# Experts' results written in quarters, the second attention's preparation moved forward, and the normed tokens stored chunk first

## The reference

```python
x = x + tanh(g_xattn[0]) * attention0(layernorm(x), ctx, ctx)
x = x + tanh(g_ffn[0])   * experts(layernorm(x))
x = x + tanh(g_xattn[1]) * attention1(layernorm(x), ctx, ctx, mask)
x = x + tanh(g_ffn[1])   * squared_relu_mix(layernorm(x))
```

```python
grouped  = x.reshape(b, s // 32, 32, d)            # 128 groups of 32 tokens in all, 16 a batch
logits   = einsum('bntd,des->bntes', grouped, Wc) + bc + tie
perm     = (logits == max over the group's tokens) # each of 128 experts picks a token of each group
permuted = einsum('bntd,bntes->bnesd', grouped, perm)
inner    = relu(einsum('bnesd,esdf->bnesf', permuted, W1) + b1)   # f = 32
result   = einsum('bnesf,esdf->bnesd', inner, W2) + b2
out      = einsum('bnesd,bntes->bntd', result, perm)
```

## Time and profile before

| | before |
|---|---|
| median of 3 runs | 1328.79 us |
| profiled execution, own time | 1330.8 us |
| its span, first to last instruction | 1329.0 us |
| PE / DVE / ACT / POOL busy | 95% / 67% / 43% / 42% |
| mean granted clock of TensorE | 0.983 of full speed |
| HBM read / written | 129.92 / 82.62 MB |

### The profile page before, as it was taken

The page is one execution under the profiler, slowest core; times in us unless marked ns, Lnnn a source line. Parts: engine busy times, 40 slices in busy tenths (PEclk is TensorE's granted clock), DMA queues, the critical chain, the costliest instruction groups (busy, mean ns, idle before and its releaser), DMA issues.

```text
span 1329.0 us, 28238 instructions
## 1 busy us (share of the span) xinstructions
PE 1258.5 (95%) x10607; PEld 905.9 (68%) x10607; DVE 887.9 (67%) x1570; ACT 571.1 (43%) x1039; POOL 553.9 (42%) x456
## 2 busy tenths in 40 slices
PE   9999999999999978887999999999997999999998
PEld 7777776777677657621446666766775778888887
DVE  6985786777666555564546766766675977777762
ACT  4255345534552554453562443344246433333331
POOL 3313642454251100000339666865834644544540
PEclk9999999999999998998899999999998999999999
DMA  9875455324421678899983653563414111111101
GB/s 350 219 184 191 154 154 174 109 80 149 141 76 33 207 207 273 287 399 362 401 340 117 221 171 94 175 220 120 131 53 159 64 63 63 63 40 54 63 27 37
DMA packets 126502, 213.59 MB, mean 161 GB/s; under 512 B 27609, under 2 KB 49369, under 8 KB 122331
## 3 DMA queue, kind: packets, MB, share of 16 engines
q1 hardware_dynamic: 126427, 212.57, 48.1%
HBM read 129.92 MB, written 82.62 MB: 160 GB/s over the span
## 4 chain that ended last, share of the span: by engine, by line
PE 76%; DVE 9%; DMA 5%; ACT 4%; issue 3%; SPq 2%; POOL 1%; ACTq 0%; DVEq 0%; POOLq 0%
PE b L157 12%; PE b L158 11%; PE b L159 11%; PE b L1585 5%; PE b L1783 5%; PE b L1784 4%; PE b L1785 4%; PE b L1557 4%; PE b L1690 3%; PE b L2113 3%; PE b L2079 3%; PE b L1698 2%; ACT a_pr L1149 2%; PE b L2097 2%; PE b L1605 2%
## 5 line engine op out<-in xcount | busy, mean ns | idle before, releaser
L1149 ACT ACTIVATE a_pr<-b 120x512 f32<-120x512 f32 x252 | 130.1, 604 | 95.3 <-PE b L1585 95.3
L1338 DVE TENSOR_REDUCE a_mx<-b 128x4 f32<-128x480 f32 x256 | 152.0, 652 | 10.3 <-PE b L1557 10.2
L1031 POOL TENSOR_TENSOR a_rp<-a_rp,a_b2s 128x512 f32<-128x512 f32 x96 | 120.4, 1290 | 24.8 <-DMA a_rp<-s_rp 24.8
L1070 POOL TENSOR_TENSOR a_atl<-a_pvs,a_ath 128x512 fp32r<-128x512 f32 x64 | 81.1, 1301 | 81.8 <-ACT a_ath L1193 81.8
L1783 PE MATMUL b<-a_woh,a_ath 128*128 128x512 f32 x256 | 105.2, 411 | 3.1 <-POOL a_atl L1070 3.1
L157 PE MATMUL b<-a_xth,a_wqh 128*128 128x512 f32 x256 | 103.7, 405 | 0.8 <-DVE a_wql L825 0.5
L1784 PE MATMUL b<-a_wol,a_ath 128*128 128x512 f32 x256 | 102.3, 400 | 0.0
L1785 PE MATMUL b<-a_woh,a_atl 128*128 128x512 f32 x256 | 102.2, 399 | 0.0
L159 PE MATMUL b<-a_xth,a_wql 128*128 128x512 f32 x256 | 101.2, 395 | 0.0
L158 PE MATMUL b<-a_xtl,a_wqh 128*128 128x512 f32 x256 | 101.1, 395 | 0.0
L1483 DVE SCALAR_TENSOR_TENSOR a_x<-b,a_gate,a_x 128x512 f32<-128x512 f32 (+1 forms) x64 | 47.8, 747 | 72.2 <-PE b L1785 72.2
(11 more groups left out here) (245 smaller groups left out, 3142.7 us busy)
## 6 DMA issues: line engine op xcount, KB each, us to landing
a_rp<-s_rp SPq DMA_DIRECT2D x128, 256.0 KB, 4.6
s_x<-a_x SPq DMA_DIRECT2D x16, 1024.0 KB, 4.3
s_rp<-e_chosen SPq DMA_DIRECT2D x16, 1024.0 KB, 7.1
s_rp<-e_xc SPq DMA_DIRECT2D x16, 1024.0 KB, 7.5
e_w<-in_w SPq DMA_DIRECT2D x56, 256.0 KB, 5.1
a_xr<-in_x_t SPq DMA_DIRECT2D x8, 1024.0 KB, 6.6
a_x<-in_x SPq DMA_DIRECT2D x8, 1024.0 KB, 10.5
s_xn<-a_xn SPq DMA_DIRECT2D x8, 1024.0 KB, 4.7
```

Of the source, the lines that this page charges most:

```text
L1031: pool.tensor_tensor(rp[:, t, a], rp[:, t, a], b2s[:, :], ALU.add).then_inc(rp_biased, 1)
L1149: act.activation(pr[:, h % RING, :], bank[k][0:S2, :], ACT.Exp, scale=SCALE)\
L1338: dve.tensor_reduce(mx[:, t, :, r], bank[k][:, 0:HJ * S2].rearrange("p (a s) -> p a s", a=HJ), AX.X, ALU.max).then_inc(free[k], 1)
```

## The change

Four things change together.

1. `s_xn` is laid out [chunk, partition, tile, 128], and the first attention's `xn` [128, chunk, tile, 128]; a quarter of a chunk is then read in pieces of 4 KB. DVE writes with strides, and the transposes and the gather's last lhs read accordingly. Chunk 2's tokens are loaded at c = 1, s = 0 to 3, after the step's block of W1, no longer at c = 0.
2. A result step takes a quarter of the groups (32, two batches): eight products with 32 rows and 32 columns, four for each of two banks. The first 8 stores are batches 0 and 1 of all experts, the other 24 the remaining three quarters by 16 experts at a time. The experts keep their natural order.
3. `load_behind`: perm of batch 0, b2 and gates at u = 5, batch 0's reads at u = 9 after the first 8 stores have landed (`front_written`), keys and `bo` at u = 11, batch 1's perm and reads at u = 31. The steps move: merge 27, weights 29, norm 32, queries 34, 36, 38, 40, maxima 36 to 43, rows 46.
4. In turn 0 of the second attention the merges of batch 1 on PE stand later: 0 and 1 after scores 2, 2 and 3 after values 1.

```diff
-MERGE_AT, WEIGHT_AT, NORM_AT, QUERIES_AT, ROWS_AT = 41, 43, 45, (47, 49, 51, 53), 58
-MAXIMA_AT = {49 + n: (n // 2, (0, 1) if n % 2 == 0 else (2, 3)) for n in range(8)}
+MERGE_AT, WEIGHT_AT, NORM_AT, QUERIES_AT, ROWS_AT = 27, 29, 32, (34, 36, 38, 40), 46
+MAXIMA_AT = {36 + n: (n // 2, (0, 1) if n % 2 == 0 else (2, 3)) for n in range(8)}
...
-        of = 0 if isinstance(j, int) and j < HALF else 1
-        src = io["rp"][of].rearrange("u (c j a t) s d -> (u c) s j t a d", c=2, a=GT, t=NT)
+        src = io["rp"].rearrange("u c j (a t) s d -> (u c) s j t a d", a=GT)
         for a in range(GT):
-            sp.dma_start(rp[:, t, a:a + 1], src[:, :, bass.ds(j - HALF * of, 1), t, a]).then_inc(rp_in[t], 16)
+            sp.dma_start(rp[:, t, a:a + 1], src[:, :, bass.ds(j, 1), t, a]).then_inc(rp_in[t], 16)
...
-        if u == 7:
+        if u == 5:
             load_perm(sp, 0)
             sp.dma_start(b2[:, :], io["b2"]).then_inc(w_in[2], 16)
             load_gates(sp)
             sp.dma_start(bq[:, :], io["bq"]).then_inc(c_in, 16)
-        if u == HALF_U:
-            front.half_written(sp)
+        if u == FRONT_U:
+            front.front_written(sp)
             for t in range(NT):
                 load_experts(sp, 0, t)
             load_query_weight(sp)
-        if u == HALF_U + 2:
+        if u == FRONT_U + 2:
             sp.wait_ge(const, 2)
             load_keys(sp, 0)
             sp.dma_start(bo[:, :], io["bo"].partition_broadcast(P)).then_inc(bo_in, 16)
-        if u == 22:
+        if u == EK - 1:
             for k, uses in TW:
                 sp.wait_ge(full[k], uses.n(None, "merge", 1) + 1)
             load_perm(sp, 1)
@@ -890,7 +888,7 @@
         if u == 28:
             load_v(sp, 0)
 
-    HALF_U = EK // 2
+    FRONT_U = EK // 4 + 1
 
     def sync(sp):
         if route:
@@ -904,7 +902,8 @@
             sp.dma_start(b2s[:, :], io["b2"]).then_inc(b2_in, 16)
...
-            sp.dma_start(tokens(io["xn_out"][i - 1]), xn[:, :, :]).then_inc(xn_st, 16)
+            sp.dma_start(io["xn_out"][:, :, bass.ds((i - 1) * NT, NT), :].rearrange("c p t d -> p c t d"),
+                         xn[:, :, :, :]).then_inc(xn_st, 16)
...
+            late = merging and first_turn(i)
+            if merging and not late:
                 merge_tile(i, i + 1, 0)
                 merge_tile(i, i + 1, 1)
             scores(i, i, 1)
-            if merging:
+            if merging and not late:
                 merge_tile(i, i + 1, 2)
             values(0)
-            if merging:
+            if merging and not late:
                 merge_tile(i, i + 1, 3)
             if merge and last_:
                 pe.wait_ge(free["t"], TB.n(B - 2, "mt", 0) + 1)
                 pe.wait_ge(free["w"], W.n(B - 2, "o", 1) + 1)
                 after[0].transposes(pe, None, (0, 1))
             scores(i, i, 2)
+            if late:
+                merge_tile(i, i + 1, 0)
+                merge_tile(i, i + 1, 1)
             values(1)
             if merge and last_:
                 after[0].transposes(pe, None, (2, 3))
+            if late:
+                merge_tile(i, i + 1, 2)
+                merge_tile(i, i + 1, 3)
...
-    def expert(k, a):
-
-        q, c = divmod(a, 2)
-        return 8 * (k // 2) + 4 * c + 2 * (k % 2) + q
+    def round_of(u):
+
+        if u < EK // 4:
+            return 0, u
+        return 1 + (u - EK // 4) % 3, (u - EK // 4) // 3
 
     def result_on_act(p, q):
 
-        return q == 0 or (p >= EK and (p % 2 == 1 or MERGE_AT < p <= NORM_AT))
+        return q == 0 or (p >= MERGE_AT and (p % 2 == 1 or MERGE_AT < p <= NORM_AT))
...
-        sp.dma_start(xc[c % 2][:, q * XQ:(q + 1) * XQ], io["xn"][q * XQ:(q + 1) * XQ].rearrange(
-            "n p d -> p n d")[:, :, c * P:(c + 1) * P]).then_inc(x_in[c % 2][q], 16)
+        tiles = slice(q * XQ, (q + 1) * XQ)
+        sp.dma_start(xc[c % 2][:, tiles], io["xn"][c, :, tiles]).then_inc(x_in[c % 2][q], 16)
...
-                if s % 2 and c + 2 < C:
-                    load_tokens(sp, c + 2, s // 2)
                 if c:
                     sp.wait_ge(h_full[s % 2], (SETS * (c - 1) + s) // 2 + 1)
                     load_w1(sp, WG * (c - 1) + s + RW)
+                if c == 1 and s < 4:
+                    load_tokens(sp, 2, s)
+                if c == 1 and s % 2:
+                    load_tokens(sp, 3, s // 2)
...
-            sp.dma_start(io["rp"][2 * u // EK][u % (EK // 2)], slot(u)).then_inc(out_st[u % RO], 16)
+            h, n = round_of(u)
+            sp.dma_start(io["rp"][n, :, 2 * h:2 * h + 2].rearrange("c j g e d -> c (j g) e d"), slot(u))\
+              .then_inc(out_st[u % RO], 16)
-    def half_written(sp):
+    def front_written(sp):
         for q in range(RO):
-            sp.wait_ge(out_st[q], 16 * (EK // 2 // RO))
+            sp.wait_ge(out_st[q], 16 * (EK // 4 // RO))
...
-            k, h = p % EK, p // EK
-            if k % 4 == 0:
-                pe.wait_ge(relued, k // 4 + 1)
-            if k % KS == 0:
-                pe.wait_ge(w2_in[k // KS], 16 * KS)
+            h, n = round_of(p // 2)
+            if h == 0 and p % 2 == 0:
+                pe.wait_ge(relued, n + 1)
+                if n % 2 == 0:
+                    pe.wait_ge(w2_in[n // 2], 16 * KS)
             for q in range(2):
-                b, n = result_bank(p, q)
-                pe.wait_ge(g_free[b], n)
-            for a in range(EJ):
-                rows, (q, c) = slice(a * EF, (a + 1) * EF), divmod(a, 2)
-                b, _ = result_bank(p, q)
-                ins = pe.matmul(gbank[b][c * NH:(c + 1) * NH, :], inner[rows, k, h * NH:(h + 1) * NH],
-                                w2[k // KS][rows, k % KS, :], start=True, stop=True, skip_group_check=True)
-                if c:
-                    ins.then_inc(g_full[b], 1)
+                b, use_of = result_bank(p, q)
+                pe.wait_ge(g_free[b], use_of)
+            for c in range(4):
+                for q in range(2):
+                    a, k = 2 * (p % 2) + q, 4 * n + c
+                    rows, (b, _) = slice(a * EF, (a + 1) * EF), result_bank(p, q)
+                    ins = pe.matmul(gbank[b][c * NQ:(c + 1) * NQ, :], inner[rows, k, h * NQ:(h + 1) * NQ],
+                                    w2[k // KS][rows, k % KS, :], start=True, stop=True, skip_group_check=True)
+                    if c == 3:
+                        ins.then_inc(g_full[b], 1)
...
-        b, n = result_bank(EK + number * KS - 1, 1)
+        last = max(u for u in range(EK) if round_of(u)[1] < 2 * number)
+        b, n = result_bank(2 * last + 1, 1)
...
-    rp_d = [dram(f"s_rp{i}", (EK // 2, P, EJ, D)) for i in range(2)]
+    rp_d = dram("s_rp", (EK // 4, 4, B, GB, EJ, D))
```

More of the change, by code:

```diff
@@ L74 @@
              ("a1_pvs", (0, 4 * KB), "f_tmp"), ("e_b1", (0, 400), "f_mu f_gate f_stats f_mv f_mark f_ve f_rstd")]
-HALF = B // 2
 Engines = namedtuple("Engines", "sync gpsimd scalar vector tensor")
@@ L593, in attention @@
         atl=([P, C, T], F32R), pvs=([P, C, T], F32), mt=([P, T], F32R), rs=([P, TQ], F32), rx=([P, TQ], F32R),
-        xn=([P, NT, D], F32), x=([P, XS, NT, D] if route else [P, XS, X_SPAN // 4], F32), xr=([P, C, T], F32), mr=([P, 2 * T], F32), wch=([P, C, ES], F32R),
+        xn=([P, C, NT, P] if route else [P, NT, D], F32), x=([P, XS, NT, D] if route else [P, XS, X_SPAN // 4], F32), xr=([P, C, T], F32), mr=([P, 2 * T], F32), wch=([P, C, ES], F32R),
         wcl=([P, C, ES], F32R), bcol=([P, 1], F32), tie=([P, G], F32), lg=([P, T], F32), gmax=([P, GB], F32),
@@ L1293, in apply @@
             for t in range(NT):
-                dve.tensor_scalar(to[:, t, :], x[:, t, :], mv[:, t, 0:1], rstd[:, t:t + 1],
+                if route:
+                    out, of = to[:, :, t, :], x[:, t, :].rearrange("p (c d) -> p c d", c=C)
+                else:
+                    out, of = to[:, t, :], x[:, t, :]
+                dve.tensor_scalar(out, of, mv[:, t, 0:1], rstd[:, t:t + 1],
                                   ALU.subtract, ALU.mult).then_inc(normed, 1)
@@ L1524, in second_norm @@
                 for t in range(NT):
-                    last = pe.transpose(bank[k][:, t * P:(t + 1) * P], xn[:, t, c * P:(c + 1) * P],
-                                        ident[:, :])
+                    last = pe.transpose(bank[k][:, t * P:(t + 1) * P], xn[:, c, t, :], ident[:, :])
                 last.then_inc(full[k], 1)
@@ L1843, in experts @@
     RB, RO, KS, RW = 6, 4, 8, 4
-    NH = NG // 2
+    NQ = NG // 4
     EARLY = 2
@@ L1933, in load_ahead @@
             tiles = slice(NTILE - 2 * NT, NTILE - NT)
-            sp.dma_start(xc[0][:, tiles], io["xn"][tiles].rearrange("n p d -> p n d")[:, :, 0:P]).then_inc(x_in[0][3], 16)
+            sp.dma_start(xc[0][:, tiles], io["xn"][0, :, tiles]).then_inc(x_in[0][3], 16)
         else:
@@ L2077, in gather @@
                 b, _ = use(SETS * c + s, a)
-                lhs = xc[c % 2][rows, TS * s + t, :] if tokens is None else tokens[rows, t, 0:P]
```

(10 more changed lines are left out.)

5 lines of the change are left out of this document (2 added, 3 removed).

## The result

The changed kernel takes 1561.51 us (median of 4 runs, 1557.83 to 1563.18), the kernel before 1329.54 beside it: a ratio of 1.1729, 95% interval 1.1702 to 1.1757. That is 232 us slower. The forecast, its range (1320 to 1341) and all four rivals missed it.

A forecast was written before the change was run, and what follows sets the result against it. PE bound the gather, the DMA queue the results stage; 560.3 - 5.9 + 28.6 + 34.2 + 28.3 + 31.5 + 13.6 + 2.1 = 692.7 for batch 1's merges, +2.5 at turn's end: median 1331.3, range 1320 to 1341 with rivals 1 to 3.

The forecast's parts named there:

- stores run at 417 GB/s, 2.51 us per MiB: Results stage: store price read from the profile before, used for the changed kernel's stores too.
- rival 3: Reads of results slow down as the HBM pitch grows from 512 KB to 1 MB: +5, median 1336; chance 0.10.
- Tokens, -5.9: Gathering: W1 load goes first, removing PE's 3.2 us wait at 496 and the low clock after it; -5.9 us together.
- A result step, 1.0 us: Results stage on PE: a step of eight 32-column products was taken to last 1.0 us, as before.
- Rival 4: Result steps: four tiles in flight is the limit, a step takes 1.9 us; +25, median 1354; chance 0.05.
- First reads at 583.0: Results stage: batch 0's reads wait for 8 stores instead of 16 and start at 583.0 instead of 610.3.
- Queue idle for 13.0 us in the query stage: Query stage: in 23.0 us the DMA queue moves only four stores, 10.0 us, leaving 13.0 us idle.
- Rival 1: Query stage: the queue never idles, merges end at 682.7; -5.5, median 1323; chance 0.24.
- PE is done at about 669, four ring slots ahead: Tail of the results stage: PE finishes its last 17 steps at about 669, ahead of the queue; before 677.4.
- Rival 2: First turn: PE waits for batch 1 and falls to the low clock; +6.5, median 1335; chance 0.23.
- Reads last, 13.6 on the path: Tail: batch 1's perm and reads, 4.46 MB, stand behind the last stores and take 13.6 us, landing at 690.6.
- Turn's end, +2.5: First turn of the second attention: merges end 4.4 us later, most of it hidden, so the turn ends +2.5 us.

The follow-up runs named there:

- flat_store: The changed kernel with results laid out quarter and round outermost in HBM, so a store's 128 rows lie behind one another; 1343.90 us, ratio 1.0099.
- odd_pitch: The changed kernel with 8 unused rows behind each part of s_rp, so a store's four blocks lie 1.0625 MB apart; 1559.12 us.
- before_outer8: The kernel before with one unused row behind each 16 rows of s_rp, so a store's destination is 8 blocks; 1411.78 us.
- flat_old_order: flat_early with the second attention's preparation back where the kernel before has it, reads behind stores 16 and 22; 1333.08 us, ratio 1.0015.
- flat_early: flat_reads_early with batch 1's merges also back in their old place in the first turn; 1338.73 us, ratio 1.0053.
- flat_reads_early: flat_store with batch 1's 16 reads issued behind store 15 instead of behind the last store; 1344.19 us, ratio 1.0094.
- before_outer16: The kernel before with one unused row behind each 8 rows of its results, so a store's destination is 16 blocks; 1338.48 us.

## Why the prediction was wrong, step by step

**The step that failed: "stores run at 417 GB/s, 2.51 us per MiB", kept for the changed kernel.** The working lists what a store has in common with the old one (evictions of the same count and size, ring slots) and carries its price over from the earlier trace rows, with which it also sizes the query stage (four stores, 10.0) and the tail (11 stores, 27.6). A store whose destination has another shape isn't the row's operation. It was no row of the trace of before, and its price should have been bounded from both sides. The trace of the changed kernel has 9.8 us. It cost 32 x 7.3 = 233 us, where 232 were lost; shown by flat_store, which restores the shape and gets 218 back. An estimate by the rule of the Trainium skill (DMA: Bandwidth & Descriptors, Why a DMA increments its semaphore by 16 and not by 1), 4 engines of 16 and thus four times 2.51, is 10.0 us a store, and the trace agrees. The forecast did look at this layout, in rival 3, and saw only the pitch and only the reads; odd_pitch shows no effect of the pitch on the stores.

The rest is read from flat_store, in which this step holds.

**Tokens, -5.9: nothing that can be measured.** Over the 8 kernels with the new layout the first result comes between 556.46 and 565.30, 561.9 in the mean; over the 6 with the old one between 560.33 and 564.37, 562.0. In flat_store it came at 559.54, not 554.4: +5.1.

The 5.9 us were read from one execution. Of the six profiled kernels with the old layout only that one and before_outer8 wait for W1 there (3.19 and 4.67 us); the other four have the low clock sooner and no such wait, and their first result comes at 561.8 in the mean, that of the two at 562.4. With the new layout the wait is gone in all eight (0.43 us at most), but PE stands idle elsewhere: the waits in its timeline from 484 to 552 us add up to 11.2 us in the mean of the eight, and to 10.8 in the mean of the six.

In flat_store the low clock was gone too (1.00 from 490 to 550), while two gathers stood for 1.34 and 1.67 us at 501 and 508, with no releaser shown (the four kernels with the old layout and no wait for W1 have one such wait each, 1.1 to 1.5 us), the gathers began 1.6 us later than before (486.64 against 485.00), and the last wait for W1 began at 550.00, where it began at 550.24 before. That wait stayed, as said (7.63 us, had 8.61). DVE's strided writes, taken as 0, show no cost: the first tokens are gathered at 488.0 us in the mean of the eight and of the six.

**A result step, 1.0 us: 0.61 where two follow each other.** Two steps, 32 records, take 1.22 us at full clock, against 1.95 for two of the old ones. Rival 4 is out, and so is four in flight as a limit. Nothing came of it. A line of flat_store's timeline of PE:

```profile
563.31 1.22 PE L2132 MATMUL b<-e_xc,e_inner 32*32 32x512 f32 x32
```

**First reads at 583.0: 591.57** in flat_store. 5.1 of it is the first result; the eight stores took 3.4 more than the 28.6 read from before. **From the reads to the first query pass 34.2: 35.1.** **Queue idle for 13.0 us in the query stage: 12.9** (0.38 of the 34 us in the window above). The agreement is partly luck: the forecast's 13.0 were idle out of 23.0 us, and 23 us from 632 to 655 have 10.4 (a share of 0.55). Rival 1 is out. The forecast's list of what is given back (13.0, 13.6, 3.5 and 1.0) comes to 31.1 us, and its own sum needs 31.7; it changes nothing here.

**"PE is done at about 669, four ring slots ahead": 681.8.** This is the second step that was wrong in kind. PE's timeline at the end of flat_store's results stage:

```profile
657.83 1.49 PE L2132 MATMUL b<-e_w,e_inner 32*32 32x512 f32 x32 [0.81 <-ACT e_xc L2027]
660.23 2.36 PE L2132 MATMUL b<-e_w,e_inner 32*32 32x512 f32 x32 [0.91 <-ACT e_chosen L2027]
...
666.76 2.36 PE L2132 MATMUL b<-e_w,e_inner 32*32 32x512 f32 x32 [0.91 <-ACT e_xc L2027]
670.03 2.36 PE L2132 MATMUL b<-e_w,e_inner 32*32 32x512 f32 x32 [0.91 <-ACT e_xc L2027]
673.29 2.36 PE L2132 MATMUL b<-e_w,e_inner 32*32 32x512 f32 x32 [0.91 <-ACT e_chosen L2027]
```

PE has nothing else left but pairs of steps with waits of 0.8 and 0.9 us for an eviction between them. Behind these waits the granted clock falls from 1.00 (655 to 660 us) to 0.50 (660 to 687), the pair goes from 1.49 to 2.36, and a store is made in 3.27 us in place of 2.40, where the queue would take one in 2.51. No eviction waits for a ring slot from 655 to 687, so the steps set the pace, and PE comes out of the stage together with the queue, not ahead of it. How much sooner the queue alone would have ended isn't shown: its share is 0.98 to 1.02 there.

With the preparation in its old place products and query passes stay mixed, and from the first result to the end of the last step it takes 115.5 us (565.30 to 680.84, flat_old_order) in place of 122.3 (559.54 to 681.79) and of 120.0 in flat_early (564.88 to 684.83). A low clock alone doesn't decide: flat_old_order stands at 0.50 from 590 to 626, where the queue is full (a share of 0.95 to 1.03), and is level with the kernel before. Rival 2, the low clock, was right as a mechanism and looked for in the wrong stage: from 693 to 704 us flat_store's clock is 1.00. Its condition, a wait of over 3 us, isn't met either where the clock did fall, behind 0.8 and 0.9.

**Reads last, 13.6 on the path: nothing comes back without them.** In flat_store the last read lands at 700.67 and the last merge starts at 700.72, so they are on its chain. But PE, late by the step before, has scores and values to do until then, and is as long a path: in flat_reads_early, which has no such reads, the last step ends 3.0 us sooner and the merges 2.8, and the time is the same (1344.19 against 1343.90; a gain of the 6 us that theory A expected at least is more than the runs leave room for). The merges end at 701.8, 9.1 after the forecast's 692.7, which is the sum 5.1 + 3.4 + 0.9 of the terms above less 0.3, and about what the profiled execution misses (1341.8 against 1333.3). From the first query pass to there it took 75.1 us where the forecast had 75.5: that is luck, since PE, which the forecast had ahead of the queue, was a second path of the same length. **Turn's end, +2.5: about +12.** Its mark is the product with the second turn's reciprocals, at 749.33 in the kernel before and at 761.51 in flat_store. Of these 12, 5.5 are POOL's row behind the late merges, by the medians of flat_reads_early and flat_early. The forecast had seen POOL "4.4 us later" and let most of it be hidden.

Open: why before_outer16 moves less over the results stage and lies 7 us above the kernel before, what the gathers wait for between 500 and 510 us with either layout, and what makes the clock fall around 490 us in some executions and not in others.

## What to carry to other kernels

A DMA's price belongs to its access patterns, not to its bytes and pieces: when a layout changes, write both patterns down, outermost dimension first, and treat one with a new outermost count as an operation that the trace doesn't show. A DMA share far under 1 while everything waits for DMA is the sign of it. And before a stage is taken apart so that one part starts sooner, ask what is left alone at its end: here the products, with waits between them and at half the clock. A gain that is read off one wait in one execution should be looked for in a second execution before it goes into a sum: here four of six didn't have it.

## What the hardware showed that was not expected

- The outermost count of a store's destination sets its rate, with the same bytes, pieces and 128 source partitions: 401 GB/s for one run of rows and for 16 blocks (one run of that kernel, and 383 against 360 over the whole stage), 202 for 8, 105 to 117 for 4. Behind stores in 4 blocks the issue of other transfers is slow too: 9.43 us for 256 KB.
- A store reads faster from more partitions, at a share of 0.97, 0.98 and 0.88: 401, 333 and 270 GB/s from 128, 64 and 32.
- Two steps of 8 products on 32 by 32 tiles overlap to 1.22 us, 0.61 us for each, with up to 16 tiles in use and each row tile on a bank of its own.
- Waits of 0.8 and 0.9 us between pairs of such steps were followed by a granted clock of 0.50, and the pair went from 1.49 to 2.36 us.
